# Third and fourth layers: the third score chunk behind the last outputs of the slot in front, the turned rows between the third and the fourth value

## The chip, the cores and the metric

The kernel runs on one core of one Trainium2 chip. A core has five engines that run side by side, each through its own list of instructions in order, and meet only through semaphores: TensorE (PE, matrix products and transposes), VectorE (DVE), ScalarE (ACT), GpSimd (POOL), and SyncE (SP), which here issues the DMA transfers. The metric is the time of one execution on the device in microseconds (us), lower is better.

## The reference

Four graph layers are applied to 128 graphs of 64 nodes with 384 features. After each comes a residual and a layer norm.

```python
x = _layernorm(x + _L0_gnn_ref(x, adj, ...))
x = _layernorm(x + _L1_gnn_ref(x, adj, ...))
x = _layernorm(x + _L2_gnn_ref(x, adj, ...))   # third layer
x = _layernorm(x + _L3_gnn_ref(x, adj, ...))   # fourth layer
```

The third and the fourth are attention with 12 heads of 32 features:

```python
# third: project the output at the end
q = x @ Wq.T; k = x @ Wk.T; v = x @ Wv.T + bv
a = softmax(q k^T * SCALE + encoding_bias)
out = (a v) @ Wo.T + bo
# fourth: biases, a mask, no projection
q, k, v = x @ Wq + bq, x @ Wk + bk, x @ Wv + bv
scores = q k^T / sqrt(32) + beta * adj, and -9e15 where adj is 0
out = softmax(scores) v
```

## The kernel before

The first two layers fill the span up to about 1640 us, and the diff doesn't touch them. Layers three and four are one function, `heads_pass`. It works in 32 **slots**, numbered n. A slot is 8 graphs, so 512 rows in T = 4 tiles of 128. Slots 0 to 15 are the third layer (`project(n)` is true), slots 16 to 31 the fourth. The 384 features are KC = 3 chunks of 128, each with four heads. Products are made of split numbers: each operand is a high part and a low part, and three products stand for one.

A slot n needs these steps:

- `rows_turned(n)`: 12 transposes on PE (L1273) turn the rows of x. They wait until both halves of x have been loaded (`x_loaded`). `high_parts` on ACT (L1440) copies each turned chunk into `hhi`, and `low_parts` on DVE (L1553) makes `hlo` from the rest.
- `query_key(n, 0..5)`: queries and keys of the three chunks, 9 products each (L1289) into the banks ring[0] and ring[1]. ACT moves them out (q: L1448 or L1450, keys: two instructions of L1453, semaphore `qk_evac`).
- `value(n, 0..3)`: values of the four tiles, 9 products each (L1297), also into ring[0] and ring[1]. DVE moves them out (`values_out`, four instructions of L1581, semaphore `v_evac`).
- `chunk_scores(n, 0..2)`: the scores of one chunk of heads (L1317, 16 products on a 64x64 part of the array, two records each in the trace) into `pair`, of which there is one. DVE takes them out in two halves (`maxima(n, k)`, L1561, then L1569 and in the third layer L1567), GpSimd takes off the maximum (L1725), ACT makes the exponential (L1463).
- `probs_turned(n, t)` (L1334), moved out by ACT (L1477), then `output(n, t)` (L1350), which DVE divides (L1603 to L1607).
- In the third layer a slot later: `outputs_turned` (L1360), split into `ohi` (ACT, L1470) and `olo` (DVE, L1613), then `result(n, 0..3)` (L1297), which DVE adds to z (`result_out`, L1619).
- `final_stats` (DVE), `final_power` (GpSimd) and `final_apply` (ACT, four instructions of L1484) are the layer norm; then SP stores z.

The order on each engine is written out by hand, and the slots are interleaved: program slot n of TensorE holds the values, third score chunk and outputs of slot n, and the turned rows, the queries and keys and two score chunks of slot n + 1.

Waits that the text below speaks of, where the code is in the quoted functions:

```python
# ACT, high_parts(n): hhi may be overwritten once ALL values of slot n-1 are made
act.wait_ge(t_done, KC * n + c + 1)
act.wait_ge(v_done, T * n)
# PE, query_key(n, k), fourth layer: the ring bank must be out of the values
pe.wait_ge(v_evac, max(T * (n - 1) + 3 + k, 0))
# PE, query_key(n, k), third layer: the bank must be out of a result
pe.wait_ge(w_evac, T * (n - 2) + (1, 4)[k])
# SP, loop over n
load_x(n + 1), load_adj(n + 1), then store(n - 1), which waits for y_done (final_apply)
```

So in SP's queue the loads of x for slot n + 2 stand behind the store of slot n - 1, and that store waits for `final_apply(n - 1)`.

Of the kernel before, what the change touches and what calls it, by code (L numbers as in the profile page):

```python
# [1107 lines left out]
def heads_pass(nc, sh, ctx, rows, groups, x_ins, x_outs, adj_d, rowvec_d, colvec_d, beta_d):  # L1108
# [6 lines left out]
    def project(n):  # L1115

        return 0 <= n < groups

    def weight(n, k):
        return SLOT[(12 if project(n) else 16) + k]  # L1120
# [141 lines left out]
    def tensor_program(pe):  # L1262
# [37 lines left out]
        def value(n, t):  # L1300
            if t < 2:
                pe.wait_ge(qk_evac, 2 * KC * n + 5 + t)
            else:
                pe.wait_ge(v_evac, T * n + t - 1)
            rows = slice(t * P, (t + 1) * P)
            row_major(lambda c: hhi[:, c, rows], lambda c: hlo[:, c, rows], weight(n, 2), ring[t % 2][:, 0:D])\
                .then_inc(v_done, 1)
# [79 lines left out]
        for n in range(slots):  # L1387
            before, more = project(n - 1), n + 1 < slots
            if n:
                value(n, 0)  # L1390
            if before:
                outputs_turned(n - 1, range(0, 2))
            if n:
                value(n, 1)
            if before:
                outputs_turned(n - 1, range(2, 4))
            value(n, 2)
            value(n, 3)
            if more:
                rows_turned(n + 1, range(KC))  # L1400
            chunk_scores(n, 2)
            if before:
                if n == 1:
                    pe.wait_ge(sh.w_ready, 16)
                for t in range(T):
                    result(n - 1, t)
            if n + 1 == groups:
                pe.wait_ge(sh.w_ready, 19)
            if more:
                query_key(n + 1, 0)  # L1410
                query_key(n + 1, 1)
            if not before and more:
                query_key(n + 1, 2)
            probs_turned(n, 0)
            if before and more:
                query_key(n + 1, 2)
            if more:
                chunk_scores(n + 1, 0)
            probs_turned(n, 1)
            if more:  # L1420
                query_key(n + 1, 3)
            output(n, 0)
            output(n, 1)
            if more:
                chunk_scores(n + 1, 1)
            probs_turned(n, 2)
            if more:
                query_key(n + 1, 4)
            probs_turned(n, 3)
            if more:  # L1430
                query_key(n + 1, 5)
            output(n, 2)
            output(n, 3)

    def scalar_program(act):
        def high_parts(n):
            for c in range(KC):
                act.wait_ge(t_done, KC * n + c + 1)
                act.wait_ge(v_done, T * n)
                nc.scalar.activation(hhi[:, c, :], row_banks[c][:, :], ACT.Copy).then_inc(hi_done, 1)  # L1440

        def query_key(n, k):
            c = k // 2
            act.wait_ge(qk_done, 2 * KC * n + k + 1)
            act.wait_ge(s_done, max(KC * (n - 1) + c + 1, 0))
            if k % 2 == 0:
                if project(n):
                    ins = nc.scalar.activation(q[:, c, :], ring[0][:, :], ACT.Copy)  # L1448
                else:
                    ins = nc.scalar.activation(q[:, c, :], ring[0][:, :], ACT.Identity, bias=colvec[:, 0, c:c + 1])  # L1450
            else:
                for h in range(2):
                    ins = nc.scalar.activation(keys[:, c, :, h, :], ring[1][:, :].rearrange("p (g j) -> p g j", j=S),  # L1453
                                               ACT.Identity, scale=halves[:, h:h + 1],
                                               bias=keycol[:, n // groups, h, c:c + 1])
            ins.then_inc(qk_evac, 1)

        def exponential(n, k):
            c, u = k // 2, k % 2
            act.wait_ge(sub_done, UNITS * n + k + 1)  # L1460
            act.wait_ge(pt_done, max(2 * T * (n - 1), 0))
            ts = slice(2 * u, 2 * u + 2)
            nc.scalar.activation(probs[n % 2][:, c, ts, :, :].rearrange("p t h j -> p h t j"), logits[:, c, :, ts, :],  # L1463
                                 ACT.Exp).then_inc(exp_done, 1)

        def outputs_high(n, ts):
            for t in ts:
                act.wait_ge(ot_done, T * n + t + 1)
                act.wait_ge(w_done, T * n)
                nc.scalar.activation(ohi[:, t, :, :].rearrange("p c j -> p (c j)"), output_banks[t][:, 0:D], ACT.Copy)\  # L1470
                    .then_inc(ohi_done, 1)

        def probs_out(n, t):
            act.wait_ge(o_done, max(T * n + t - 1, 0))
            for half in range(2):
                act.wait_ge(pt_done, 2 * (T * n + t) + half + 1)
                nc.scalar.activation(probt[t % 2][:, PAIRS // 2 * half:PAIRS // 2 * (half + 1), :]  # L1477
                                     .rearrange("p m i -> p (m i)"), pt[half][:, 0:PAIRS // 2 * P], ACT.Copy)\
                    .then_inc(pt_evac, 1)

        def final_apply(n):
            act.wait_ge(fb_done, n + 1)
            for t in range(T):
                ins = nc.scalar.activation(z[n % 2][:, t, :], z[n % 2][:, t, :], ACT.Identity, scale=FR[:, t:t + 1],  # L1484
                                           bias=FB[:, t:t + 1])
            ins.then_inc(y_done, 1)

        high_parts(0)
        yield
        act.wait_ge(cleared, 2)  # L1490
        query_key(0, 0)
        query_key(0, 1)
        yield
        for k in range(2, 2 * KC):
            query_key(0, k)
        yield
        for k in range(2):
            exponential(0, k)
        for a in range(2):
            act.wait_ge(rows.stored[a], 16 * (groups // 2))  # L1500
        for n in range(slots):
            before, more = project(n - 1), n + 1 < slots
            if n + 1 == groups:
                act.wait_ge(col_in, 16 * 3)
                act.wait_ge(cleared, 5)
            if before:
                outputs_high(n - 1, range(T))
            if more:
                high_parts(n + 1)
            if n == 0:  # L1510
                exponential(0, 2)
                exponential(0, 3)
            if before or not more:
                exponential(n, 4)
                exponential(n, 5)
                if more:
                    query_key(n + 1, 0)
                    query_key(n + 1, 1)
                probs_out(n, 0)
                if more:  # L1520
                    query_key(n + 1, 2)
            else:
                query_key(n + 1, 0)
                exponential(n, 4)
                query_key(n + 1, 1)
                exponential(n, 5)
                query_key(n + 1, 2)
                probs_out(n, 0)
            probs_out(n, 1)
            if more:  # L1530
                query_key(n + 1, 3)
                exponential(n + 1, 0)
            probs_out(n, 2)
            if more:
                exponential(n + 1, 1)
                query_key(n + 1, 4)
            probs_out(n, 3)
            if n:
                final_apply(n - 1)
            if more:  # L1540
                query_key(n + 1, 5)
                exponential(n + 1, 2)
                exponential(n + 1, 3)
        final_apply(slots - 1)

    def vector_program(dve):
# [3 lines left out]
        def low_parts(n):  # L1550
            for c in range(KC):
                dve.wait_ge(hi_done, KC * n + c + 1)
                nc.vector.tensor_tensor(hlo[:, c, :], row_banks[c][:, :], hhi[:, c, :], ALU.subtract).then_inc(lo_done, 1)  # L1553
# [113 lines left out]
        for n in range(slots):  # L1667
            before, more = project(n - 1), n + 1 < slots
# [11 lines left out]
            values_out(n, 2)  # L1680
            if n == 0:
                maxima(0, 2)
            values_out(n, 3)
            if more:
                low_parts(n + 1)
            if n == 0:
                maxima(0, 3)
                for a in range(2):
                    dve.wait_ge(rows.stored[a], 16 * (groups // 2))
# [237 lines left out]
```

## Time and profile before

| what | value |
|---|---|
| median of 3 runs | 2738.29 us (2735.63 to 2738.45) |
| the profiled execution's own time | 2736.33 us |
| its span | 2734.5 us |
| PE busy | 2648.5 us, 97% of the span |
| DVE busy | 1958.8 us, 72% |
| POOL busy | 1403.7 us, 51% |
| ACT busy | 1245.4 us, 46% |

The span is the time from the first to the last instruction of the profiled execution; its own time is 1.8 us longer. The times below are us from the start of the span.

### The profile page before, as it was taken

Reading aid. Unit: us, or ns where it says so; the run is one execution under the profiler, and the core shown is the slowest. Engines: PE = TensorE matmul, PEld = TensorE weight load, DVE = VectorE, ACT = ScalarE, POOL = GpSimd, SP = SyncE. Lnnn points to the kernel's source line nnn. Section 1 sums busy time; section 2 is a strip of 40 time slices with the busy share of each in tenths; the row PEclk is TensorE's granted clock in tenths of the full one; section 3 lists DMA queues with packets and bytes.
Section 4 is the critical chain, followed back from the end, with each engine's and each line's share of the span. In section 5 each row is a group of like instructions: output and inputs, shape, how many; then the busy total and the mean of one; then the engine's idle time right before and its main releaser. Section 6 shows DMA issues by size and latency. Waiting matters only on the chain.

```text
span 2734.5 us, 60161 instructions
## 1 busy us (share of the span) xinstructions
PE 2648.5 (97%) x23616; PEld 2298.8 (84%) x23616; DVE 1958.8 (72%) x4530; ACT 1245.4 (46%) x2433; POOL 1403.7 (51%) x1287
## 2 busy tenths in 40 slices
PE   7999999999977999999999998999999999999997
PEld 7998999899966788888888877888888888888886
DVE  5788888888873556555655668887787777767775
ACT  2344344444332344444444444445544445555554
POOL 6656755755755666666666655332233223333343
PEclk9999999999988999999999999999999999999998
DMA  5012111121113111111111121111111111112111
GB/s 157 32 42 67 55 52 56 58 77 31 59 47 116 48 47 59 32 41 53 43 35 53 44 69 44 51 52 51 46 32 51 51 51 52 52 58 70 52 52 61
DMA packets 152425, 150.29 MB, mean 55 GB/s; under 512 B 74704, under 2 KB 150096, under 8 KB 152144
## 3 DMA queue, kind: packets, MB, share of 16 engines
q1 hardware_dynamic: 152144, 146.45, 17.7%
q8 instruction: 188, 3.08, 0.5%
q14 instruction: 93, 0.76, 0.1%
HBM read 96.09 MB, written 50.33 MB: 54 GB/s over the span
## 4 chain that ended last, share of the span: by engine, by line
PE 65%; DMA 1%; POOL 1%; DVE 1%; issue 1%; ACT 0%; POOLq 0%; ACTq 0%; SPq 0%; DVEq 0%
PE bank L289 15%; PE bank L1289 14%; PE bank L1297 10%; PE bank L273 4%; PE pair L273 4%; PE bank L1350 4%; PE pair L1317 4%; PE bank L1334 3%; PE bank L302 2%; PE bank L1273 2%; PE bank L259 1%; PE bank L317 1%; PE pair L317 1%; PE bank L1360 1%; DMA h_xa<-x 1%
## 5 line engine op out<-in xcount | busy, mean ns | idle before, releaser
L1725 POOL TENSOR_TENSOR h_logits<-h_logits,h_mx 128x512 f32<-128x512 f32 x192 | 202.1, 1053 | 497.7 <-DVE h_mx L1569 497.7
L945 DVE TENSOR_TENSOR l_val<-l_ring,l_vec 64x384 f32<-64x384 f32 x512 | 284.6, 556 | 75.4 <-PE l_ring L758 68.4
L758 PE MATMUL l_ring<-whi,l_hhi 128*128 128x384 f32 x1152 | 275.9, 347 | 5.8 <-POOL wlo L69 5.8
L758 PE MATMUL l_ring<-wlo,l_hhi 128*128 128x384 f32 x1152 | 263.7, 337 | 0.0
L758 PE MATMUL l_ring<-whi,l_hlo 128*128 128x384 f32 x1152 | 263.4, 336 | 0.0
L1289 PE MATMUL bank<-h_hhi,whi 128*128 128x512 f32 x576 | 238.9, 415 | 0.4 <-ACT h_q L1448 0.2
L1289 PE MATMUL bank<-h_hlo,whi 128*128 128x512 f32 x576 | 227.5, 395 | 0.0
L1289 PE MATMUL bank<-h_hhi,wlo 128*128 128x512 f32 x576 | 227.0, 394 | 0.0
L758 PEld LDWEIGHTS l_ring<-whi,l_hhi 128*128 128x128 f32 x1152 | 199.0, 189 | 30.4 <-issue 18.6
L353 ACT ACTIVATE l_sides<-bank 128x512 f32<-128x512 f32 x192 | 114.2, 595 | 210.2 <-PE bank L289 210.2
L1581 DVE TENSOR_TENSOR h_val<-bank,h_rowvec 64x192 f32<-64x192 f32 x512 | 181.7, 355 | 37.0 <-PE bank L1297 28.0
L758 PEld LDWEIGHTS l_ring<-wlo,l_hhi 128*128 128x128 f32 x1152 | 206.8, 188 | 0.0
L758 PEld LDWEIGHTS l_ring<-whi,l_hlo 128*128 128x128 f32 x1152 | 206.3, 188 | 0.0
L1035 POOL TENSOR_TENSOR l_hlo<-l_hf,l_hhi 128x576 fp32r<-128x576 f32 x96 | 134.4, 1428 | 117.7 <-ACT l_hhi L872 117.7
L1453 ACT ACTIVATE h_keys<-bank,h_keycol,h_halves 128x512 f32<-128x512 f32 x192 | 138.7, 775 | 81.1 <-PE bank L1289 81.1
L1074 POOL TENSOR_TENSOR l_vdiag<-l_vdiag,l_vec 128x384 f32<-128x384 f32 x128 | 126.7, 1009 | 67.8 <-ACT l_vdiag L853 67.0
L415 DVE TENSOR_TENSOR l_val<-bank,l_vec 128x384 f32<-128x384 f32 x64 | 35.7, 557 | 170.8 <-PE bank L273 170.5
L1477 ACT ACTIVATE h_probt<-bank 128x384 f32<-128x384 f32 x256 | 111.4, 489 | 68.1 <-PE bank L1334 68.0
L1569 DVE TENSOR_REDUCE h_mx<-h_logits 128x8 f32<-128x512 f32 x192 | 130.9, 682 | 3.3
L1289 PEld LDWEIGHTS bank<-h_hhi,wlo 128*128 128x128 f32 x576 | 107.9, 187 | 26.7
L1289 PEld LDWEIGHTS bank<-h_hhi,whi 128*128 128x128 f32 x576 | 108.3, 188 | 24.2 <-issue 3.7
L1289 PEld LDWEIGHTS bank<-h_hlo,whi 128*128 128x128 f32 x576 | 108.6, 188 | 19.2
(234 smaller groups left out, 6694.0 us busy)
## 6 DMA issues: line engine op xcount, KB each, us to landing
l_hf<-xt SPq DMA_DIRECT2D x16, 864.0 KB, 4.9
l_x<-x SPq DMA_DIRECT2D x16, 768.0 KB, 4.5
l_x<-x SPq DMA_DIRECT2D x32, 384.0 KB, 3.2
h_xa<-x SPq DMA_DIRECT2D x32, 384.0 KB, 5.1
h_xb<-x SPq DMA_DIRECT2D x32, 384.0 KB, 5.1
x<-l_zfa SPq DMA_DIRECT2D x8, 768.0 KB, 3.5
x<-l_zfb SPq DMA_DIRECT2D x8, 768.0 KB, 4.3
x<-l_za SPq DMA_DIRECT2D x8, 768.0 KB, 3.6
```

Source lines behind the costliest of these rows:

```text
L273: mm = nc.tensor.matmul(value_bank(n, k)[:, 0:D], hh[:, c, k * P:(k + 1) * P], ww[:, c, :], start=(j == 0), stop=(j == len(terms) - 1))
L289: mm = nc.tensor.matmul(ring[k % RING][:, :], ww[:, c, m * P:(m + 1) * P], hh[:, c, :], start=(j == 0), stop=(j == len(terms) - 1))
L758: mm = nc.tensor.matmul(ring[k % RING][:, 0:D], hh[:, c, first:first + P], ww[:, c, :], start=(j == 0), stop=(j == len(terms) - 1))
L945: ins = nc.vector.tensor_tensor(val[half, (g + b) % GRAPHS, 0:D], ring[k % RING][half, 0:D], bias[half, :], ALU.add)
L1035: nc.gpsimd.tensor_tensor(hlo[:, c, :], hf[:, c, :], hhi[:, c, :], ALU.subtract).then_inc(lo_done, 1)
L1074: nc.gpsimd.tensor_tensor(vdiag[:, t, 0:D], vdiag[:, t, 0:D], vec[:, n % 4 // 2, 1, :], ALU.add)\
L1289: mm = nc.tensor.matmul(ring[k % 2][:, :], ww[:, c, m * P:(m + 1) * P], hh[:, c, :], start=(c == 0 and j == 0), stop=(c == KC - 1 and j == 2))
L1297: mm = nc.tensor.matmul(out, lhs, rhs, start=(j == 0), stop=(j == len(terms) - 1))
L1453: ins = nc.scalar.activation(keys[:, c, :, h, :], ring[1][:, :].rearrange("p (g j) -> p g j", j=S), ACT.Identity, scale=halves[:, h:h + 1] ...
L1569: nc.vector.tensor_reduce(mx[:, c, :, ts], row, AX.X, ALU.max)\
L1581: ins = nc.vector.tensor_tensor(val[S * p:S * p + S, 2 * t + b, :, p, 0:HD], src[rows, :, p, :], bias[rows, :, p, :], ALU.add)
L1725: nc.gpsimd.tensor_tensor(row, row, mx[:, c, :, ts].unsqueeze(3).broadcast_to([P, HP, 2, S]), ALU.subtract).then_inc(sub_done, 1)
```

## The change

Groups of instructions change their place; no work is added or taken away.

```diff
@@ tensor_program @@
             value(n, 2)
-            value(n, 3)
             if more:
                 rows_turned(n + 1, range(KC))
-            chunk_scores(n, 2)
+            value(n, 3)
+            if n == 0:
+                chunk_scores(0, 2)
...
             output(n, 2)
             output(n, 3)
+            if more:
+                chunk_scores(n + 1, 2)
@@ scalar_program @@
             probs_out(n, 3)
+            if more:
+                query_key(n + 1, 5)
             if n:
                 final_apply(n - 1)
             if more:
-                query_key(n + 1, 5)
                 exponential(n + 1, 2)
                 exponential(n + 1, 3)
@@ vector_program @@
             values_out(n, 2)
             if n == 0:
                 maxima(0, 2)
-            values_out(n, 3)
             if more:
                 low_parts(n + 1)
+            values_out(n, 3)
```

The next rows are each engine's list of instructions, the way the program holds it. `x12` counts instructions in a row. Lines of the changed program are 3 or 4 higher than those of the program before.

TensorE, fourth layer, from the last outputs of a slot to the first value of the next; before:

```order
L1289 MATMUL bank<-h_hhi,wlo 128x512
L1350 MATMUL bank<-h_val,h_probt_11300 64x66 x12
L1350 MATMUL bank<-h_val,h_probt_11301 64x66 x12
L1297 MATMUL bank<-whi,h_hhi 128x384 x3
L1297 MATMUL bank<-wlo,h_hhi 128x384 x3
L1297 MATMUL bank<-whi,h_hlo 128x384 x3
```

The same place in the changed program:

```order
L1289 MATMUL bank<-h_hhi,wlo 128x512
L1350 MATMUL bank<-h_val,h_probt_11300 64x66 x12
L1350 MATMUL bank<-h_val,h_probt_11301 64x66 x12
L1317 MATMUL pair<-h_keys,h_q 64x2x64 x16
L1297 MATMUL bank<-whi,h_hhi 128x384 x3
L1297 MATMUL bank<-wlo,h_hhi 128x384 x3
L1297 MATMUL bank<-whi,h_hlo 128x384 x3
```

The score chunk (L1317) now follows the outputs and stands ahead of the values.

TensorE, fourth layer, from the fourth value (three rows of L1297) to the first query of the next slot (L1289); before:

```order
L1297 MATMUL bank<-whi,h_hhi 128x384 x3
L1297 MATMUL bank<-wlo,h_hhi 128x384 x3
L1297 MATMUL bank<-whi,h_hlo 128x384 x3
L1273 MATMUL bank<-ident,h_xb 128x128 x12
L1317 MATMUL pair<-h_keys,h_q 64x2x64 x16
L1289 MATMUL bank<-h_hhi,whi 128x512
```

The same place in the changed program, from the turned rows on:

```order
L1273 MATMUL bank<-ident,h_xb 128x128 x12
L1297 MATMUL bank<-whi,h_hhi 128x384 x3
L1297 MATMUL bank<-wlo,h_hhi 128x384 x3
L1297 MATMUL bank<-whi,h_hlo 128x384 x3
L1289 MATMUL bank<-h_hhi,whi 128x512
```

The fourth value now stands between the turned rows and the query; before, turned rows and score chunk stood there. In the third layer the four results stand between the fourth value and the query.

ScalarE, fourth layer, end of a slot; before, `final_apply` (x4) ahead of the last keys (L1453):

```order
L1463 ACTIVATE h_probb<-h_logits 128x4x2x64
L1450 ACTIVATE h_q<-bank,h_colvec 128x512
L1477 ACTIVATE h_probt_11301<-bank 128x384 x2
L1484 ACTIVATE h_zb<-h_zb,h_small 128x384 x4
L1453 ACTIVATE h_keys<-bank,h_keycol,h_halves 128x8x64 x2
L1463 ACTIVATE h_probb<-h_logits 128x4x2x64 x2
```

And in the changed program:

```order
L1466 ACTIVATE h_proba<-h_logits 128x4x2x64
L1453 ACTIVATE h_q<-bank,h_colvec 128x512
L1480 ACTIVATE h_probt_11301<-bank 128x384 x2
L1456 ACTIVATE h_keys<-bank,h_keycol,h_halves 128x8x64 x2
L1487 ACTIVATE h_za<-h_za,h_small 128x384 x4
L1466 ACTIVATE h_proba<-h_logits 128x4x2x64 x2
```

The keys went ahead of the layer norm's last step, whose end releases the store in SP's queue.

## Rows read from the trace of the kernel before

**Rows 1.** Page: busy time of the engines

```profile
PE 2648.5 (97%) x23616; PEld 2298.8 (84%) x23616; DVE 1958.8 (72%) x4530; ACT 1245.4 (46%) x2433; POOL 1403.7 (51%) x1287
```

**Rows 2.** Windows in the third and fourth layer: length, busy us, granted clock, DMA

```profile
1700.00:2270.00 570.00, 570.00 (x5638) 502.74 (x5637) 448.92 (x1018) 281.28 (x521) 172.26 (x168) 1.00 0.15 46
2320.00:2690.00 370.00, 368.39 (x3879) 311.02 (x3878) 268.89 (x640) 205.35 (x369) 137.60 (x135) 1.00 0.19 57
```

**Rows 3.** Chain that ended last, a fourth-layer slot: start, us, what

```profile
2459.31 6.76 PE bank L1297 x36
...
2467.50 1.03 PE pair L1317 x32
...
2481.18 1.09 PE pair L1317 x32
...
2487.94 1.55 PE bank L1350 x48
```

**Rows 4.** The same chain, a third-layer slot

```profile
1977.74 1.77 PE bank L1297 x9
...
1980.17 1.57 PE bank L1297 x9
...
1985.53 1.31 PE bank L1273 x12
...
1987.88 6.45 PE bank L1297 x36
1994.32 4.18 PE bank L1289 x18
...
2013.52 1.55 PE bank L1350 x48
```

**Rows 5.** Timeline of ACT, fourth layer: start, us, instructions [idle before]

```profile
2466.66 1.58 ACT L1440 ACTIVATE h_hhi<-bank 128x512 fp32r<-128x512 f32 x3 [5.42 <-PE bank L1273]
...
2479.67 1.44 ACT L1453 ACTIVATE h_keys<-bank,h_keycol,h_halves 128x512 f32<-128x512 f32 x2 [1.50 <-PE bank L1289]
...
2486.54 2.50 ACT L1484 ACTIVATE h_za<-h_za,h_small 128x384 f32<-128x384 f32 x4
```

**Rows 6.** Timeline of SP's queue: stores of z (L1226), both layers

```profile
2014.56 0.37 SPq L1226 DMA_DIRECT2D x<-h_za  x1
...
2489.07 0.38 SPq L1226 DMA_DIRECT2D out<-h_za  x1
```

**Rows 7.** Line L1217, window 2017.2 to 2017.5: second load behind the store

```profile
L1217 SPq DMA_DIRECT2D h_xb<-x x1: 504/504/504, 2017.1 to 2017.1; - x1
...
DMA to landing us min/median/max: 4.5/4.5/4.5
```

**Rows 8.** Line L1273, window 1700 to 2734: what ended PE's idle time

```profile
DMA h_xa<-x: 3.1, 6
DMA h_xb<-x: 2.7, 5
```

**Rows 9.** Timeline of DVE, fourth layer: the low parts

```profile
2467.60 1.89 DVE L1553 TENSOR_TENSOR h_hlo<-bank,h_hhi 128x512 fp32r<-128x512 f32 x3
```

**Rows 10.** Timeline of DVE, third layer: values out, low parts, result_out

```profile
1984.41 2.94 DVE L1581 TENSOR_TENSOR h_val<-bank,h_rowvec 64x192 f32<-64x192 f32 x8
1987.38 1.89 DVE L1553 TENSOR_TENSOR h_hlo<-bank,h_hhi 128x512 fp32r<-128x512 f32 x3
...
1993.48 1.51 DVE L1619 TENSOR_TENSOR h_za<-bank,h_za 128x384 f32<-128x384 f32 x3
```

**Rows 11.** Timeline of PE, behind two long idle times [in brackets]

```profile
891.26 0.55 PE L317 MATMUL bank<-l_val,l_dt 64*64 64x385 f32 x1 [3.37 <-DVE l_dt L431]
...
1654.44 1.10 PE L1317 MATMUL pair<-h_keys,h_q 64*64 64x128 f32 x32 [3.47 <-DVE h_logits L1561]
```

**Rows 12.** Windows behind them: granted clock is third from the end

```profile
891.00:896.00 5.00, 4.74 (x23) 2.58 (x24) 3.28 (x12) 1.75 (x4) 0.00 (x0) 0.66 0.86 200
1655.00:1658.00 3.00, 3.00 (x31) 2.38 (x24) 2.80 (x6) 0.76 (x2) 2.32 (x3) 1.00 0.00 0
```

## The prediction

> **What bounds the kernel now.** I read the page first: TensorE is busy for 97% of the span, the next engine for 72% [rows 1]. Then the windows of the two layers that the change touches: in 570 us of the third layer TensorE is busy for all 570, in 370 us of the fourth for 368.4, both at full granted clock [rows 2]. The chain that ended last is there little else than TensorE's own instructions, one behind the other [rows 3, 4]. So these slots go at TensorE's rate: moving work can gain only what a change between kinds of products costs, and each new wait counts in full, once a slot. The question is which cover each moved piece gave away. I write E for the moment at which the last output of a slot ends (2459.31 in the fourth-layer slot, 1977.74 in the third-layer one) and count from there. The next E are 2487.94 + 1.55 and 2013.52 + 1.55, so slots of 30.2 and 37.3 us.
>
> **Part 1, TensorE's order alone.** Nine products of a value take 1.77 us behind outputs and 1.57 elsewhere; four results behind a score chunk take 6.45, not 4 x 1.57 = 6.28 [rows 4]. A score chunk takes 1.03 behind turned rows and 1.09 behind outputs [rows 3]. Before, a slot pays 0.20 (outputs to value) and 0.17 (scores to result); after, 0.06 (outputs to scores) and 0.17 (scores to value): a gain of 0.14. In the fourth layer four values take 6.76, 0.28 more than 6.28 + 0.20: the third and the fourth wait for `values_out`. The fourth no longer would, 0.14 more. Over 31 and 15 slots: -6 us. The last value now stands behind turned rows, as the second stands behind turned outputs now, at 1.57 [rows 4].
>
> The moved scores need the last keys. Scores 1 have the same distance already: their keys are out at 2479.67 + 1.44 = 2481.11 [rows 5], the outputs end and the scores start at 2481.18 [rows 3]. So I cost this at nothing. The cover is the 1.55 us of outputs; without the edit on ScalarE `final_apply` would add its 2.50 here.
>
> **Part 2, the loads of x.** This is what the edit on ScalarE costs. `final_apply` now ends before E, at 2486.54 + 2.50 = 2489.04 [rows 5], and SP issues the store at 2489.07 [rows 6]. After the change the keys go first. Their product ends at E - 1.55, they are out at E, `final_apply` ends at E + 2.4, and the store goes out at E + 2.43, where it now does at E - 0.4. Queued behind it are both loads of x for the rows turned in the slot that has just begun. From the store to the second landing the third layer has 2014.56 [rows 6] to 2017.1 + 4.5 = 2021.6 [rows 7], 7.05 us; I take 7.1. After the change x is there at E + 9.5.
>
> The Trainium skill (DMA: Bandwidth & Descriptors, sections Bandwidth and Latency and other measured facts) has about 2 us fixed and some 358 GB/s; as an estimate from the page the 1.5 MB are in after 6.3 us, not 7.1. By it each wait would be 0.8 us shorter, 22 us over 28 slots. The row decides.
>
> In the fourth layer the turned rows would be due at 1.09 + 0.20 + 3 x 1.57 + 0.14 = 6.15 behind E: a wait of 3.4 us. They now wait 5.8 us in all [rows 8], 0.39 a slot. In the third layer they are due at 7.25 (1.09, and 1985.53 - 1977.74 less a value and the gain at the switch): a wait of 2.25. `store` also releases GpSimd's residual of the third layer; that is late by the same 2.8 us and is not asked for until the next slot's results, so nothing.
>
> **Part 3, the high and low parts.** `high_parts(n + 1)` waits for all values of slot n. Now the turned rows stand behind the last value, and ScalarE starts at 2466.66, 0.6 us into them [rows 5]. After the change it starts only behind value 3, whatever the rows do. From the end of value 3 to the first query: 0.2 us to ScalarE, 0.6 for the first high part (three take 1.58 [rows 5]), 0.63 for the first low part (three take 1.89 [rows 9]), 0.2 for the hand-overs, together 1.6. Before, this lay under 1.31 of turned rows and 1.03 of scores.
>
> *Fourth layer, query 0 straight behind value 3.* Rows from 9.5, value 3 from 10.85 to 12.5, query 0 from 14.1. `values_out(n, 3)` stands behind the low parts, which end at 15.35; it takes 1.5 (2.94 for two [rows 10]), so key 0, whose bank it frees, starts at 17.0, not 16.2, and ends at 19.1. Before: query 0 at 2467.50 + 1.03 - 2459.31 = 9.2, both done 4.2 later [rows 3, 4], with the 0.39 at 13.8. I add 0.1, since the exponentials reach ScalarE later. Cost: 5.4 us a slot, 14 slots (17 to 30): 75.6.
>
> *Third layer, four results in between.* Rows from 9.5, value 3 to 12.4. VectorE works there from the low parts at 1987.38 to the last `result_out` at 1993.48 + 1.51 = 1994.99, 7.61 us [rows 10], and key 0 starts at 1994.32 + 2.09 = 1996.4 [rows 4], 1.4 us later. After the change the low parts start at 12.4 + 0.85 = 13.25 and a `values_out` of 1.47 comes in behind them: 13.25 + 7.61 + 1.47 = 22.3. Key 0, whose bank the last result must leave, starts at 22.45; it started at 18.65. TensorE alone would be there at 20.8. Cost: 3.8 us, 14 slots (2 to 15): 53.2. The results, 6.3 us, hide the rest of the delay; they end in the fourth layer, whose price shows it.
>
> *Other slots.* Slot 1 has no store ahead of its load: 1.6. Slot 0 keeps a score chunk behind value 3: 1.0. Slot 16 has results, but less to do on VectorE: 2.7. In slot 31 a score chunk of 1.1 goes ahead of the values that VectorE waits for, and that chain sets the end: 1.1.
>
> **The sum.** 75.6 + 53.2 + 1.6 + 1.0 + 2.7 + 1.1 = 135 us (part 1 is in the positions used) on the profiled execution's own 2736.3: 2871. The median of the runs is 2 us higher: 2873.
>
> **The clock.** The new waits of 3.4 us in the fourth layer are as long as two idle times in the trace, 3.37 and 3.47 us [rows 11]. Behind the first the granted clock is 0.66 over 5 us, so it was for a while at the lower level, 1.2 GHz, and 1.7 us of work were lost; behind the second it stayed at 1.00, 2.4 GHz [rows 12]. I count the loss in half of the 14 slots: 12 us. The forecast is 2885.
>
> **Rivals.**
> 1. *Every wait for x takes the clock down.* Then turned rows and value 3, 2.9 us, go at half rate in each of the 14 slots: 41 us on 2873, so 2914, and up to 2940 with some of the third layer's waits. For it: the window at 891. Against: the one at 1655. The Trainium skill (TensorE: Matmul & The Clock Gate, HAM oscillation) describes a kernel whose clock falls at the data wait of every tile; by that rule this rival holds. 15%.
> 2. *The loads land some 2 us earlier,* because less else is under way. Then 28 slots give back 2 each: 2817 without clock losses. Against: in the third layer the same store and loads are already alone. 14%.
> 3. *The loads cost nothing, only part 3 shows,* if the store goes out as early as now: third-layer slots cost 1.6, fourth-layer ones 2.1, with the others 2790. Against: ScalarE and SP's queue both go in order. 5%.
> 4. *The other side: faster.* The mechanism is part 1: fewer changes between 64-row and full products, -6 us, and the 5 us of waits for x gone as well, 2728, 0.4% faster. It decides only if x lands before E + 6.15 and the high parts of a slot can start before its last value ends. The quoted waits speak against both. 2%.
> 5. *No effect,* gains and losses both too small to show: 2%.
>
> The forecast has 62%. The range of 8 in 10 goes from 2815 to 2935: down to rival 2 and over rival 1's first figure. Under 0.2% a measurement of this kernel can't tell from no change; faster 2%, within 3%, slower 95%.
>
> **What would show it.** In the changed kernel's trace: PE L1273 idle on DMA of x, about 30 us in the third layer and 47 in the fourth; the store issued at E + 2.4; L1289 idle on the low parts, 1.6 us in each fourth-layer slot, and on the values' move for 0.7; in the third layer L1289 idle on `h_z`, 1.5 to 2 a slot; L1317 behind the outputs with no wait; slots of 41.1 and 35.6 us. The prediction is wrong if x lands by E + 7, if VectorE has the last values out earlier than I have it, or if the clock is down through most of the fourth layer.

## The result and the profile after

| | kernel before | changed kernel |
|---|---|---|
| median | 2736.96 us (2734.78 to 2738.45, 4 runs) | 2892.99 us (2892.55 to 2897.34, 4 runs) |
| span of the profiled execution | 2734.5 us | 2891.3 us |

The changed kernel is slower: ratio 1.0574, 95% interval 1.0556 to 1.0593. The forecast was 2885 us, the range 2815 to 2935. Of the runs below, one execution of e6 (4415 us) and one of e8 (12837 us) were in a slow state; they are in those two medians and in no ratio.

Page of the changed kernel, busy time of the engines, the line that answers to [rows 1]:

```profile
PE 2687.2 (93%) x23616; PEld 2316.0 (80%) x23616; DVE 1955.9 (68%) x4530; ACT 1242.8 (43%) x2433; POOL 1403.6 (49%) x1287
```

The work is the same, but TensorE's share fell from 97 to 93%, and it is busy 39 us longer for the same instructions. A lower clock does that, and idle times do some of it: e1 below, at full clock, is busy 13 us longer (2661.4). The windows in the two layers, as [rows 2] (length, busy us of each engine with its instructions, granted clock, DMA share, GB/s):

```profile
1700.00:2350.00 650.00, 598.06 (x5776) 516.57 (x5774) 459.28 (x1044) 287.40 (x534) 178.37 (x172) 0.99 0.15 43
2400.00:2840.00 440.00, 381.96 (x3817) 317.58 (x3816) 262.96 (x624) 199.92 (x360) 135.06 (x133) 0.96 0.16 48
```

TensorE now idles 8% of the third layer and 13% of the fourth, where it idled 0 and 0.4%. What it waited for, in the third layer (window 1700 to 2350; us in total, times, longest):

```profile
PE bank L1273 <- DMA h_xb<-x: 17.5, 8, 3.4
PE bank L1273 <- DMA h_xa<-x: 14.7, 7, 2.6
PE bank L1289 <- DVE h_zb L1623: 8.9, 15, 1.0
PE bank L1289 <- DVE h_za L1623: 8.4, 13, 1.0
```

and in the fourth (window 2350 to 2860):

```profile
PE bank L1273 <- DMA h_xb<-x: 22.8, 7, 4.0
PE bank L1289 <- DVE h_hlo L1557: 22.2, 14, 1.8
PE bank L1273 <- DMA h_xa<-x: 21.9, 7, 3.3
```

The turned rows (L1273) wait 2.1 us for x in each third-layer slot and 3.2 in each fourth-layer slot; the first query (L1289) waits 1.6 for the low parts in the fourth layer, and in the third the query and key 0 wait together 1.2 for `result_out`. The chain of one fourth-layer slot, the answer to [rows 3] (start, us, what; "issue" is time with nothing visible), follows the order of part 2 of the prediction:

```profile
2562.59 0.77 ACT h_keys L1456
2563.36 2.40 ACT h_zb L1487 x4
...
2565.78 0.38 SPq L1226
...
2566.28 0.44 SPq L1217
...
2566.82 5.87 DMA h_xa<-x
...
2572.73 2.12 PE bank L1273 x12
2574.85 2.60 PE bank L1297 x9
...
2577.53 0.61 ACT h_hhi L1443
...
2578.16 1.01 DVE h_hlo L1557 x2
```

Keys, then `final_apply`, then the store, then the loads, then the landing at 2572.69, 6.9 us behind the store. Only then TensorE works again, and at once it is slow: 12 turned rows take 2.12 us and a value 2.60, against 1.31 and 1.57 [rows 4], and against 1.53 and 1.59 behind the wait in the third layer, where the clock stays up. The third-layer slot, the answer to [rows 4], shows the same head and VectorE's chain behind it:

```profile
2055.37 0.37 SPq L1226
...
2056.33 6.01 DMA h_xb<-x
2062.39 1.53 PE bank L1273 x12
2063.91 1.59 PE bank L1297 x9
2065.59 0.61 ACT h_hhi L1443
2066.22 1.02 DVE h_hlo L1557 x2
...
2073.88 1.41 DVE h_zb L1623 x3
2075.33 2.35 PE bank L1289 x9
```

Slot lengths are read from store to store in SP's queue, for instance (timeline of SP's queue):

```profile
2055.37 0.37 SPq L1226 DMA_DIRECT2D x<-h_za  x1
2096.59 0.37 SPq L1226 DMA_DIRECT2D x<-h_zb  x1
...
2528.73 0.38 SPq L1226 DMA_DIRECT2D out<-h_za  x1
2565.78 0.38 SPq L1226 DMA_DIRECT2D out<-h_zb  x1
...
2639.67 0.38 SPq L1226 DMA_DIRECT2D out<-h_zb  x1
2675.12 0.38 SPq L1226 DMA_DIRECT2D out<-h_za  x1
```

Third-layer slots take 41.2 us (37.3 before). Of 14 fourth-layer slots (30.2 before) three take 35.35 to 35.49 and eleven 36.8 to 38.1.

### The profile page after: what moved, and what is told of

It is laid out like the page before. It is cut to its first block, busy times and chain, and to the rows that moved or that the text cites. A ratio compares the mean times of both kernels' runs of the same rounds, so it can differ in the third digit from the quotient of the medians.

```text
span 2891.3 us, 60161 instructions
## 1 busy us (share of the span) xinstructions
PE 2687.2 (93%) x23616; PEld 2316.0 (80%) x23616; DVE 1955.9 (68%) x4530; ACT 1242.8 (43%) x2433; POOL 1403.6 (49%) x1287
## 4 chain that ended last, share of the span: by engine, by line
PE 51%; DVE 6%; DMA 6%; ACT 4%; issue 2%; SPq 1%; POOL 0%; ACTq 0%; DVEq 0%; POOLq 0%
PE bank L289 14%; PE bank L1289 12%; PE bank L273 4%; PE pair L273 3%; PE bank L1334 3%; DMA h_xb<-x 3%; DMA h_xa<-x 3%; PE bank L1297 3%; PE pair L1317 2%; PE bank L302 2%; PE bank L1273 2%; PE bank L1350 2%; DVE h_hlo L1557 2%; DVE h_val L1585 1%; PE bank L259 1%
## 5 line engine op out<-in xcount | busy, mean ns | idle before, releaser
L1289 PE MATMUL bank<-h_hhi,whi 128*128 128x512 f32 x576 | 244.5, 424 | 43.1 <-DVE h_hlo L1557 22.2
L1289 PE MATMUL bank<-h_hlo,whi 128*128 128x512 f32 x576 | 228.8, 397 | 0.0
L1289 PE MATMUL bank<-h_hhi,wlo 128*128 128x512 f32 x576 | 228.0, 396 | 0.0
L1289 PEld LDWEIGHTS bank<-h_hhi,whi 128*128 128x128 f32 x576 | 109.1, 189 | 85.2 <-issue 28.5
L1557 DVE TENSOR_TENSOR h_hlo<-bank,h_hhi 128x512 fp32r<-128x512 f32 x96 | 60.4, 685 | 163.5 <-ACT h_hhi L1443 163.5
L1443 ACT ACTIVATE h_hhi<-bank 128x512 fp32r<-128x512 f32 x96 | 50.5, 599 | 260.8 <-PE bank L1297 257.8
```

The source lines that it names most:

```text
L1289: mm = nc.tensor.matmul(ring[k % 2][:, :], ww[:, c, m * P:(m + 1) * P], hh[:, c, :], start=(c == 0 and j == 0), stop=(c == KC - 1 and j == 2))
```

## The experiments

Times are medians; each run has its own runs of the kernel before beside it, 2735.0 to 2737.0 us. Slot lengths are from the trace, as above, and are those of most slots; the first two of the third layer and a few others are longer.

| run | median us | ratio to before (95%) | third-layer slot | fourth-layer slot |
|---|---|---|---|---|
| changed kernel | 2892.99 | 1.0574 (1.0556 to 1.0593) | 41.2 | 35.4 or 37.0 |
| e1 loads ahead of the store | 2789.25 | 1.0192 (1.0177 to 1.0207) | 39.0 | 32.1 |
| e2 keys behind final_apply | 2820.61 | 1.0305 (1.0289 to 1.0320) | 39.9 | 33.1 to 33.7 |
| e3 rows back | 2783.39 | 1.0170 (1.0155 to 1.0185) | 37.9 | 32.55 |
| e4 wait filled | 2875.91 | 1.0513 (1.0496 to 1.0531) | 41.2 | 35.5 |
| e5 second place for hhi, hlo | 2871.59 | 1.0494 (1.0480 to 1.0508) | 41.2 | 34.5 to 36.1 |
| e6 low parts behind values_out | 2913.53 | 1.0647 (1.0627 to 1.0666) | 40.5 | 37.3 to 40.0 |
| e9 e4 and e6 | 2894.83 | 1.0576 (1.0561 to 1.0592) | 40.5 | 37.4 |
| e10 rows and low parts only | 2794.45 | 1.0210 (1.0194 to 1.0225) | 38.0 to 39.6 | 32.2 to 33.3 |
| e11 e1 and e5 | 2761.66 | 1.0091 (1.0074 to 1.0107) | 39.0 | 30.05 |
| e12 e11, scores out early | 2734.30 | 0.9992 (0.9983 to 1.0001) | 37.3 | 30.05 |
| e7 before, loads ahead of the store | 2732.15 | 0.9990 (0.9981 to 0.9998) | 37.3 | 30.1 |
| e8 e7, scores moved in the third layer | 2731.51 | 0.9983 (0.9974 to 0.9992) | 37.3 | 30.1 |

### Is it the store in front of the loads? (e1)

```diff
 load_x(n + 1, half)      # both halves
+if n > 1:
+    store(n - 2)
 sync.wait_ge(s_evac, UNITS * n)
 load_adj(n + 1)
-store(n - 1)
...
-store(slots - 1)
+for m in range(3, 0, -1):
+    store(slots - m)
```

> The changed kernel, with one more move: in SP's queue the store of slot n-2 stands behind the loads of x for slot n+1, not ahead of them. Theory (the store that waits for final_apply holds the loads back): in the third layer the turned rows wait no longer, a slot costs 1.6 us over the kernel before (part 3 alone); in the fourth the rows wait only for x that is loaded once GpSimd has used it, so they start at about E + 6.6 and a slot costs 2.4; the granted clock stays up, since the longest idle time is 1.6 us. Sum 22 + 34 + 6 = 62 on 2737: about 2799 us. Rival A (VectorE's order sets the slot and the wait for x only lies beside it): no gain in the third layer, its slots stay at 41.2 us, total 2850 or more. Rival B (the clock falls because of the waits of part 3 too): about 2815, with windows of 0.95 in the fourth layer.

Measured 2789.25 us, 104 under the changed kernel, with no wait for x left in the list of waits. That speaks against rival A. Rival B falls too: the granted clock is 1.00 from 2400 to 2700 us (rival B wanted 0.95), with the parts' own waits as long as before:

```profile
PE bank L1291 <- DVE h_hlo L1559: 22.2, 14, 1.9
PE bank L1291 <- DVE h_za L1625: 9.6, 15, 0.9
PE bank L1291 <- DVE h_zb L1625: 9.0, 15, 0.9
```

The expectation was 10 us too high, most of it because fourth-layer slots take 32.1 us where 32.6 was expected: the rows were to wait a little for x, and do not wait. The loads land 2.9 to 4.1 us after their issue there (L1217, window 2540 to 2640), where they took 3.8 to 5.2 behind the store in the kernel before (window 2458 to 2492).

### The edit on ScalarE alone (e2)

```diff
 probs_out(n, 3)
-if more:
-    query_key(n + 1, 5)
 if n:
     final_apply(n - 1)
 if more:
+    query_key(n + 1, 5)
```

> The changed kernel with the edit on ScalarE undone: final_apply stands ahead of the last keys again. Theory: the store is issued at E - 0.4 again and x lands in time, but the moved scores wait for their keys, which are out at about E + 0.95. That is a wait of 1.0 a slot, with which turned rows are due later than x lands. A fourth-layer slot costs 3.0 over the kernel before, a third-layer slot 2.5, together 42 + 35 + 6 = 83: 2820 us. Rival, as the prediction put the price of the cover: final_apply adds its whole 2.5 to each slot, 1.5 more in 28 slots: 2862 us. Rival 2 (the wait for x does not come from final_apply's place): the L1273 wait for DMA stays near 2.7 us a slot and the time goes over 2893.

Measured 2820.61 us. The waits of TensorE:

```profile
PE pair L1317 <- ACT h_keys L1456: 27.1, 30, 1.0
...
PE bank L1273 <- DMA h_xa<-x: 1.3, 4, 0.4
PE bank L1273 <- DMA h_xb<-x: 0.8, 2, 0.4
```

The scores wait 0.9 a slot for their keys and the rows hardly for x. So the edit that the change made to protect the scores saves 0.9 us a slot there and costs 2.1 to 3.2 at the rows; without it the change would have been 72 us less slow.

### Turned rows back (e3), and turned rows alone (e10)

```diff
 value(n, 2)
+value(n, 3)
 if more:
     rows_turned(n + 1, range(KC))
-value(n, 3)
```

On VectorE e3 also puts `values_out(n, 3)` ahead of `low_parts(n + 1)` again.

> The changed kernel with turned rows behind value 3 again, and the low parts behind the last values_out again; the scores and the edit on ScalarE stay as changed. Theory: the loads still land at E + 9.5, but the rows are due 1.6 us later, at 7.75 in the fourth layer and 8.9 in the third, so they wait 1.7 and 0.6; the high and low parts lie under the rows again. A fourth-layer slot costs 1.95, a third-layer slot 0.6 over the kernel before, together 27 + 8 + 4: about 2776 us, and the clock stays up. Rival (most of the loss is the moved store, not the rows' place): fourth-layer slots still cost 3.4 or more, total over 2800.

Measured 2783.39 us. Third-layer slots are as expected (37.9), fourth-layer slots 0.4 longer (two more, 34.2 and 34.7, apart): the rows are due later, but the query follows the high and the low part of their first chunk, 2.2 us behind the landing, so the landing still sets the slot. The chain there:

```profile
2555.11 5.99 DMA h_xa<-x
...
2561.14 0.67 PE bank L1273 x4
...
2561.84 0.61 ACT h_hhi L1443
...
2562.47 0.70 DVE h_hlo L1557
...
2563.31 6.52 PE bank L1289 x27
```

e10 does the opposite: it makes only this part of the change, in the kernel before, and leaves the scores and ScalarE as they were (VectorE has the low parts ahead of `values_out(n, 3)`):

```diff
 value(n, 2)
-value(n, 3)
 if more:
     rows_turned(n + 1, range(KC))
+value(n, 3)
 chunk_scores(n, 2)
```

> Only one part of the change: turned rows ahead of value 3 and low parts ahead of its values_out. The score chunk stands behind value 3, where it was, and final_apply ahead of the last keys. Theory: x lands at E + 6.6 as in the kernel before, but the rows are due at 5.05 in the fourth layer, a wait of 1.5, and at 6.15 in the third, 0.45; the scores cover 1.0 of the 1.6 behind value 3; key 0 waits for the values' move. A fourth-layer slot costs 2.25 over the kernel before, a third-layer slot 0.95, together 31 + 13 + 5 on 2735: about 2785 us. Rival (the scores between value 3 and the query cover the parts altogether, as they seem to in the kernel before): about 2755 us.

Measured 2794.45 us, against the rival by 40, and 9 over the theory. The low parts are waited for 0.55 a slot in the fourth layer, as expected. The wait for x is 19.8 us in the fourth layer, 1.4 a slot for the 1.5 expected, but 11.2 in the third, 0.8 a slot for 0.45. There the chain runs over `final_apply`, a second load whose issue takes 2.0 us, and its landing. So this part alone costs 58 us.

### Did the clock lengthen eleven of the slots? (e4)

```diff
 value(n, 2)
 if more:
+    if n >= groups:
+        pe.wait_ge(v_evac, T * n + 2)
+        for _ in range(2):   # the products of value 3, overwritten later
+            row_major(..., weight(n, 2), ring[1][:, 0:D])
     rows_turned(n + 1, range(KC))
 value(n, 3)
```

> The changed kernel with 18 more products ahead of the turned rows in each fourth-layer slot: value 3 made twice for nothing, into its own bank, which it overwrites afterwards. The output is the same. They take 3.1 us and lie in the wait for x of 3.3. Theory (in 11 of 14 fourth-layer slots the clock falls behind that wait and turned rows and value 3 lose 1.5 us): the granted clock stays at 1.00, every fourth-layer slot takes 35.4 to 35.7 us, and the time falls by 11 x 1.5 = 17 to about 2876 us. Rival (the longer slots have another cause, such as the transfer itself): no gain, 2893 or a little more.

Measured 2875.91 us: 18 more products in each of 15 slots (16 to 30), and the kernel is 17 us faster than the changed one. The window in its fourth layer has the granted clock at 1.00 (2.4 GHz), where the changed kernel has 0.96:

```profile
2400.00:2820.00 420.00, 399.45 (x3974) 336.66 (x3975) 256.25 (x607) 195.76 (x353) 132.33 (x130) 1.00 0.17 50
```

Eleven of 14 fourth-layer slots take 35.4 to 35.5 us and one 35.6. Of the other two, the one of 36.84 shows that the wait for x isn't the only one that counts: its clock fell to 0.50 behind a wait of 1.8 us for the low parts (windows of 2 us from 2744 on). The Trainium skill (TensorE: Matmul & The Clock Gate, HAM oscillation) says that a kernel with a data wait in every tile gets a clock that falls in every tile; here it fell in eleven of 14 slots. From the turned rows to the first query, TensorE takes 4.67 us in the three slots at full clock and 1.4 to 2.6 us more in ten of the others; in the eleventh the clock fell only behind the wait for the low parts, and the query took 3.7 us for 2.5. Together that is 18 us.

### Is the wait for all values the reason for part 3? (e5)

From slot 18 on, even slots keep their parts in `ohi` and `olo`, which the fourth layer leaves free:

```diff
-act.wait_ge(v_done, T * n)
-nc.scalar.activation(hhi[:, c, :], ...)
+act.wait_ge(v_done, T * (n - 1) if n > groups + 2 else T * n)
+nc.scalar.activation(parts(n)[0][:, c, :], ...)
```

> The changed kernel, order as changed; the high and low parts of every second fourth-layer slot from slot 18 on lie in the memory of ohi and olo, which the fourth layer doesn't use. So from slot 18 on high_parts waits for the values of the slot in front of the last, not of the last. Theory (part 3: the price behind value 3 comes from that wait): the parts are made under value 3, the first query follows it without the wait of 1.6 on h_hlo and key 0 without the 0.6 on h_val; the wait for x stays at 3.3. A fourth-layer slot falls by 2.3, from 37.0 to 34.7 (33.1 where the clock stays up), 13 slots: 30 us, about 2863. Rival (the low parts, not the wait for the values, are late, because VectorE is busy with values_out): h_hlo is waited for still, gain under 10 us.

Measured 2871.59 us, 21 less. No wait for `h_hlo` is left (one of 1.6 for `h_olo`, in slot 17, ahead of the remedy), and in the chain the query follows the value directly:

```profile
2627.16 5.91 DMA h_xa<-x
...
2633.12 2.74 PE bank L1282 x12
2635.86 2.00 PE bank L1307 x9
2637.86 6.30 PE bank L1299 x27
```

So the mechanism holds and the rival falls. The gain is 9 us short, 1.6 a slot for 2.3. Most of that is the clock (0.94 over the fourth layer): behind the same wait for x it now falls in every slot, also in those in which it stayed up before. From the turned rows to key 0 these slots take 6.3 to 7.9 us, where e11 below, with the same parts and no wait for x, takes 5.0.

### The order on VectorE (e6 and e9)

```diff
 values_out(n, 2)
+values_out(n, 3)
 if more:
     low_parts(n + 1)
-values_out(n, 3)
```

> The changed kernel with VectorE's edit undone: values_out of the fourth value stands ahead of the low parts again. Theory: in the fourth layer nothing changes in sum, the query waits for the low parts 0.8 longer and key 0 no longer for the values. In the third layer the copy now fills time in which VectorE waited for the high parts, its chain is 0.6 us shorter, 14 slots: 9 us, about 2884. Rival (the order on VectorE was needed): the query's later start is not given back, fourth-layer slots cost 0.8 more and the total is 2900 or more.

Measured 2913.53 us: a miss by 30. The third layer did what was expected in most slots (40.5 for 41.2), but three took 42.1 to 42.2: behind waits for x of 2.0 to 2.1 us the granted clock was 0.66 over 5 us. Fourth-layer slots became 2.0 longer (38.8 for 36.8 on average). Three windows from one of them: the first begins in the wait for x, the second ends in the wait for the low parts, the third holds the query:

```profile
2652.00:2657.00 5.00, 2.75 (x13) 2.75 (x14) 0.62 (x2) 0.00 (x0) 0.00 (x0) 0.71 0.39 126
2657.00:2660.00 3.00, 1.90 (x10) 1.57 (x8) 1.04 (x3) 1.00 (x3) 0.00 (x0) 0.92 0.00 0
2660.00:2665.00 5.00, 3.73 (x10) 3.03 (x11) 4.88 (x10) 0.57 (x2) 1.05 (x1) 0.66 0.00 0
```

The clock is at the lower level twice in the slot. e9 puts e4's filling into this order, to see which of the waits does it.

> e4's additional products (value 3 twice for nothing in the wait for x, fourth layer) together with e6's order on VectorE (values_out of the fourth value ahead of the low parts). In e6 the trace showed the granted clock at the lower level twice in a fourth-layer slot, behind the wait for x and behind the wait of 2.4 for the low parts. Theory (the order on VectorE costs nothing by itself, the clock made e6 slower): with the first wait filled the clock stays up, fourth-layer slots take 35.5 us as in e4, third-layer slots 40.55 as in e6, together 2876 - 9 = 2867 us. Rival A (the wait of 2.4 takes the clock down by itself): the clock falls once in a slot, slots of 37.3, about 2893 us. Rival B (the order costs time at full clock): slots of 36.3 or more with the clock at 1.00.

Measured 2894.83 us, rival A's figure. The wait for x is filled and the clock stays up there, but the wait for the low parts takes it down by itself. Waits and chain of that kernel:

```profile
PE bank L1289 <- DVE h_hlo L1561: 33.2, 14, 2.4
```

```profile
2643.03 1.60 PE bank L1297 x9
2646.99 8.08 PE bank L1289 x27
```

A value at full rate (1.60), an idle time of 2.4, and 27 products in 8.08 us, which take 6.49 in the kernel before. That is so in 12 of the 14 slots; in one where the clock stayed up the slot took 35.62 us. So one wait of 2.4 us is dearer than the changed kernel's two, 1.6 for query 0 and some 0.4 for key 0: this order of VectorE costs 1.9 us a slot against e4, nearly all of it by the clock.

### Both remedies, and the rest (e11, e12)

e11 is the changed order with e1's and e5's edits.

> The changed kernel with both remedies: loads of x ahead of the store (e1) and a second place for the high and low parts in the fourth layer (e5). Theory (the store in front of the loads and the wait for all values are all that the fourth layer lost): fourth-layer slots from 19 on take 30.1 us again, third-layer slots stay at 39.0 as in e1, where VectorE's chain sets them: 2789 - 13 x 2.0 = 2763 us. Rival (a third cost in the fourth layer, such as ScalarE's later exponentials): slots of 30.6 or more, 2770 or more.

Measured 2761.66 us, fourth-layer slots of 30.05. So the fourth layer had lost nothing else, and 131 of the 156 us are back. What is left is the third layer; e12 goes at it on VectorE:

```diff
 values_out(n, 2)
+if n and project(n):
+    maxima(n, 4)
 if more:
     low_parts(n + 1)
 values_out(n, 3)
 ...
-maxima(n, 4)
+if n == 0 or not project(n):
+    maxima(n, 4)
```

> e11, and in the third layer VectorE takes out the first half of the third score chunk (maxima(n, 4), 1.9 us) ahead of the low parts, in the time in which it waits for the high parts. Theory (what is left in the third layer is VectorE's chain from the low parts to the last result_out, which holds key 0 back): the chain is 1.9 us shorter, the wait for h_z goes, third-layer slots take 37.2 to 37.4 us for 39.0 in e11, fourth-layer slots stay at 30.05. 15 x 1.7 under e11: 2736 us, level with the kernel before. Rival (TensorE's wait for h_z has another source, such as the results themselves): third-layer slots stay at 38.5 or more, over 2750 us.

Measured 2734.30 us. TensorE's waits for `result_out` in e11 (in total, times, longest):

```profile
PE bank L1301 <- DVE h_za L1636: 9.6, 15, 1.0
PE bank L1301 <- DVE h_zb L1636: 9.0, 15, 1.0
```

and what is left of them in e12:

```profile
PE bank L1301 <- DVE h_zb L1636: 0.3, 1, 0.3
```

Third-layer slots take 37.3 us again. With three remedies the changed order is level with the kernel before.

### Anything to gain for the kernel before? (e7, e8)

e7 is the kernel before with e1's edit.

> The kernel before with the one move of e1: the loads of x stand ahead of the store in SP's queue. e1 had no wait for x left. Theory (the second load lands late because it shares the DMA engines with the store): the 5.8 us that TensorE waits for x in the fourth layer go, nothing else changes: 2731 us, 0.2% faster. Rival (those waits come from the late use of x by GpSimd alone): the same time as before, waits of 5 to 6 us stay.

Measured 2732.15 us, ratio 0.9990 (0.9981 to 0.9998). The waits for x are gone from its list, and fourth-layer slots are 30.1 throughout. e8 adds the moved score chunk and the keys ahead of `final_apply` in slots of the third layer:

```diff
-chunk_scores(n, 2)
+if n == 0 or not project(n):
+    chunk_scores(n, 2)
...
 output(n, 3)
+if more and project(n + 1):
+    chunk_scores(n + 1, 2)
```

> e7, and in the third layer alone the moved score chunk with the keys ahead of final_apply; turned rows and low parts where they were, the fourth layer as before. Theory (part 1: fewer changes between kinds of products are worth 0.14 us a slot, and with the loads ahead of the store no new wait comes with them): 15 slots x 0.14 = 2 us under e7, 2729 us, third-layer slots of 37.2. Rival (e3's third-layer slots, 0.55 us longer than before with a wait for x of which 0.6 is known, hide a further cost on VectorE): third-layer slots of 37.5 or more, 2735 or more.

Measured 2731.51 us, ratio 0.9983 (0.9974 to 0.9992). Against e7 that is 0.6 us, within the noise of either; the traces have third-layer slots of 37.27 against 37.33, 0.06 less where I had 0.14.

## Why the prediction was right

**The loads of x (part 2)** were the largest term, and it held: store at E + 2.4, second landing 6.9 us later (7.1 taken), waits of 3.2 in the fourth layer (3.4) and 2.1 in the third (2.25), 45 and 32 us in all (47 and 30). e1 shows that the place in SP's queue is the cause: 104 us come back, a share of them through the clock. The estimate worked out from the Trainium skill (DMA: Bandwidth & Descriptors, sections Bandwidth and Latency and other measured facts), 6.3 us, was 0.6 under the trace. That ended rivals 2 and 3: the loads did not land 2 us earlier than taken, and they were not hidden. Rival 3's 2790 leaves out the 6.4 us of the other slots that it names; with them it is 2796, and e1, which is nearly its case, measured 2789.

**The high and low parts (part 3)** held in both layers. In the fourth, query 0 waits 1.6 us as taken, and e5 shows the reason. Key 0 was priced too high: 0.8 taken, some 0.4 measured, since query 0 starts 2.47 us ahead of it and 2.10 in e11. The 0.6 a slot that the trace puts down to the values' move is the wait of key 0's weight load, not of its products:

```profile
PEld bank L1289 <- DVE h_val L1585: 7.5, 13, 0.6
```

In the third layer VectorE's chain was right to 0.1 us a slot, 41.2 against 41.1, and e12 shows that it is that chain; TensorE's waits for it are 1.2 a slot, under the 1.5 to 2 named as a sign.

**The clock** was the term mis-sized. I counted 7 slots at 1.7 us, 12 us. That half was a choice between two cases in the trace, one for each side, and not worked out. The trace has eleven of 14 and 18 us, and e4 gives 17 us. The other errors partly cancel. Also over the forecast are the first two intervals between stores, 42.6 and 43.4 us, by 3.7 us: the first has a wait for x of 3.4 where 2.25 was taken, in the second the clock is down as well. The twelve after them are over by 2.3, one of them taking 42.8, and slot 16 by 1.4. Under it are the 14 fourth-layer slots, by some 2.5 without the clock. Together that is about the 10 us by which the profiled execution, 2893.05 us, is over 2871 + 12; by the medians it is 8. Rival 1 was nearer in frequency, but not in price: the clock was down for only part of the 2.9 us of work that it named.

**TensorE's own order (part 1)** was too small to matter and mis-sized as well: 0.14 us a slot forecast, 0.06 measured in e8. The sentence that without the edit on ScalarE `final_apply` would add its 2.50 to the scores was wrong: e2 shows 0.9, since `final_apply` lies for the most part beside the last key's products and had already ended before E.

Rival 4, faster, fell as argued. It needed x by E + 6.15 and parts that start before the last value ends. e11 and e12 supply just these, and then the order is level, not faster.

## What to carry to other kernels

When an instruction is put behind another on one engine, follow its end into every queue that waits for it. Here 2.8 us on an engine with 46% load delayed a store, the store two loads behind it in the same queue, and the loads the engine that had no slack. A wait on a buffer that frees late ("all values of the slot in front") is invisible while other work lies over it; count that cover before moving it. And put loads that the next stage needs ahead of a store that can wait; here its buffer was not needed until a slot later.

## What the hardware showed

A short wait in each slot costs more than itself when it takes TensorE's clock down. In the changed kernel's fourth layer the granted clock fell behind ten of 14 idle times of 3.0 to 4.0 us, and once behind the 1.8 us that followed another. In e9 it fell behind 12 of 14 idle times of 2.4 (27 products in 8.08 us for 6.49). Behind 1.6 in e4 and about 2.0 in most third-layer slots it stayed at 1.00, but not in all: e4 has a fall behind 1.8, and e6 three behind 2.0 to 2.1. So in these runs the length of the idle time alone doesn't tell whether the clock falls. Useless products in the wait made the kernel 17 us faster. Which pattern of idle and busy time decides was not tried further.
